# Slot tiles of a mixture-of-experts stage gathered by a list of tokens, in place of scattered and read back

## The reference

```python
def _L1_ffn_ref(x, w12, w3, router_w, expert_bias, sw1, sw2, sw3):   # E = 8, TOPK = 2
    g = x @ sw1.T                                   # shared expert, 1024 hidden
    u = x @ sw2.T
    shared_out = silu(g) * u @ sw3.T
    scores = sigmoid(x @ router_w.T)
    _, top_idx = top_k(scores + expert_bias, TOPK)
    top_scores = take_along_axis(scores, top_idx, axis=-1)
    top_scores = top_scores / (top_scores.sum(-1, keepdims=True) + 1e-09)
    combine = zeros((T, E)).at[arange(T)[:, None], flat_idx].add(flat_sc)
    h12 = einsum('td,ehd->teh', flat_x, w12)        # every expert: 128 hidden
    h1, h2 = split(h12, 2, axis=-1)
    out_e = einsum('teh,edh->ted', silu(h1) * h2, w3)
    return shared_out + einsum('ted,te->td', out_e, combine)
```

## Time and profile before

| | us |
|---|---|
| median of 3 runs | 472.29 (470.79 to 473.45) |
| profiled execution, its own time | 470.29 |
| its span, first to last instruction | 468.2 |
| TensorE busy in the span | 345.0 (74%) |
| VectorE busy | 322.6 (69%) |
| ScalarE busy | 256.0 (55%) |
| GpSimd busy | 101.4 (22%) |
| mean granted clock of TensorE | 0.874 of full speed |

### The profile page before, as it was taken

How to read it: one execution, slowest core, us unless ns; L and a number is a source line. 1 busy time by engine, 2 the same in 40 slices (tenths; PEclk the granted TensorE clock), 3 DMA queues, 4 the chain that set the end, 5 groups by cost and what they waited for, 6 DMA issues and landing times. The chain is left out here.

```text
span 468.2 us, 10194 instructions
## 1 busy us (share of the span) xinstructions
PE 345.0 (74%) x4018; PEld 270.8 (58%) x4018; DVE 322.6 (69%) x730; ACT 256.0 (55%) x527; POOL 101.4 (22%) x152
## 2 busy tenths in 40 slices
PE   1999778876599958252027788975999779888971
PEld 1544467765477747231026545654888677777861
DVE  5799997797416673999994368687895445542556
ACT  2879784466446782666223357657862336553241
POOL 6394000600000012200007400030077100003730
PEclk9999989897999997755559959997899789999986
DMA  7798000000000000000000000000012440222322
GB/s 217 243 353 294 0 0 1 0 2 0 0 3 1 3 3 1 0 1 1 0 0 3 4 3 6 3 1 1 1 45 102 132 162 1 91 104 88 99 60 90
DMA packets 18954, 24.84 MB, mean 53 GB/s; under 512 B 2582, under 2 KB 17068, under 8 KB 18860
## 3 DMA queue, kind: packets, MB, share of 16 engines
q1 hardware_dynamic: 17372, 19.99, 13.2%
q0 software_dynamic: 1536, 4.20, 2.8%
HBM read 18.02 MB, written 9.18 MB: 58 GB/s over the span
## 5 line engine op out<-in xcount | busy, mean ns | idle before, releaser
L1520 PE MATMUL ps<-ident,area 128*128 128x128 f32 x32 | 8.3, 409 | 40.6 <-DVE area L1850 40.6
L2198 PE MATMUL ps<-down_r,hidden_r 128*128 128x256 f32 x192 | 30.8, 320 | 6.7 <-DVE hidden_r L2498 3.8
L2198 PEld LDWEIGHTS ps<-down_r,hidden_r 128*128 128x128 f32 x192 | 29.4, 226 | 8.8 <-DVE hidden_r L2498 4.3
L2408 POOL DMA_INDIRECT stored<-results_dram,slots x16 | 16.7, 1045 | 67.4 <-DMA results_dram<-stored 62.8
L1520 PEld LDWEIGHTS ps<-ident,area 128*128 128x128 f32 x32 | 5.3, 202 | 43.4 <-DVE area L1850 43.4
L1847 DVE TENSOR_TENSOR third<-area 128x124 f32<-128x124 f32 (+15 forms) x31 | 29.3, 944 | 1.1
L1850 DVE TENSOR_TENSOR area<-area,third 128x124 f32<-128x124 f32 (+15 forms) x31 | 27.9, 901 | 1.1
L2230 PE MATMUL ps<-routed_up,xm_r 128*128 x138 | 23.4, 307 | 5.6 <-DVE stored L2510 2.7
L2182 PE MATMUL ps<-xm_r,gate_r 128*128 128x512 f32 x96 | 26.0, 407 | 1.0 <-ACT stored L2332 0.7
L1692 ACT ACTIVATE area<-ps,own_side 128x512 f32<-128x512 f32 (+1 forms) x16 | 15.9, 1100 | 19.1 <-PE ps L1520 19.1
L1748 ACT COPY area<-third 32x128 f32<-32x128 f32 x64 | 18.9, 295 | 13.1 <-DVE third L1894 11.9
(11 more groups left out here) (386 smaller groups left out, 987.4 us busy)
## 6 DMA issues: line engine op xcount, KB each, us to landing
stored<-in_L_ffn_sw_dram SPq DMA_DIRECT2D x3, 1024.0 KB
stored<-in_L_ffn_w_dram SPq DMA_DIRECT2D x1, 2048.0 KB
results_dram<-stored SPq DMA_DIRECT2D x2, 1024.0 KB, 4.5
stored<-rows_dram SPq DMA_DIRECT2D x1, 1920.0 KB, 8.0
x<-L_attn_hidden_state_dram SPq DMA_DIRECT2D x4, 256.0 KB, 3.6
out_dram<-x SPq DMA_DIRECT2D x4, 256.0 KB, 2.2
rows_dram<-L_attn_hidden_state_dram SPq DMA_DIRECT2D x1, 896.0 KB
stored<-rows_dram SPq DMA_DIRECT2D x1, 768.0 KB, 5.0
```

The source lines that it names most:

```text
L1520: last = nc.tensor.transpose(ps[:, bank, i * P:(i + 1) * P], inv[:, r].rearrange("p q c -> p (q c)"), ident[:])
L2198: last = nc.tensor.matmul(ps[:, t // 2, t % 2 * D:(t % 2 + 1) * D], hidden_r[:, n % 2, hp, t * P:(t + 1) * P], down_r[:, wp, a, :], start= ...
L2408: nc.gpsimd.indirect_dma_start(found[:, k, t, :], None, core.results_dram, bass.IndirectOffsetOnAxis(slots[:, k, t:t + 1], 0)) \
```

## The change

The scatter, `rows_dram`, its fill and the read-back go. In their place:

- SyncE stores `xm` to `xm_dram` (1 MB) as soon as it is normalised.
- VectorE makes two sets of 0/1 masks: `map_slots` (step 2) marks for each token and choice in which slot tile it lies (`of_tile`, multiplied by the token's number), `spread_places` (step 3) marks at which row of that tile (`in_tile`, 16 x 128 wide).
- TensorE multiplies them (`list_tokens`, step 5): 16 matmuls of 23 columns give, for each row of each slot tile, the number of its token; `keep_list` copies it to `token_of`. Padding rows get token 0, a finite row.
- GpSimd issues 23 indirect DMAs, each of which gathers a slot tile straight into SBUF, the places in a ring of 16 tiles. Tiles 16 to 22 reuse the places of tiles 0 to 6, so GpSimd waits ahead of tile 16 until results 0 to 7 have been stored (`FIRST_OUT`). TensorE waits for the gathered tiles in four parts: 0 to 3, 4 to 9, 10 to 15, 16 to 22.
- EARLY becomes 8: step 8 is computed behind the slot tiles. The weight groups are spread over steps 1 to 7, weighing moves to step 6, `keep_first` to j = 4, and one more tile is combined at the last step.

```diff
-    STEPS, EARLY, LAG = B * SH, 9, 3
-    ROW_PARTS = (0, 2, NT)
-    RESULT_PARTS = ((0, 8), (8, 16), (16, 20), (20, SLOTS))
+    STEPS, EARLY, LAG = B * SH, SH, 3
+    ROW_PARTS = (0, 4, 10, 16)
+    RESULT_PARTS = ((0, NT), (NT, 2 * NT), (2 * NT, 20), (20, SLOTS))
...
+        place = spare[:, P + 4 * NT * E + SLOTS * E:][:, 0:P]
+        RING = 2 * NT
+        rows = core.stored[:, 0:RING * D].rearrange("p (i d) -> p i d", d=D)
+        in_tile = core.stored[:, 0:2 * NT * P].rearrange("p (a r) -> p a r", a=2 * NT)
+        reached, of_tile = (core.stored[:, (NT + 2 * k) * D:(NT + 2 * k) * D + 2 * NT * (SLOTS + 1 - k)]
+                            .rearrange("p (a j) -> p a j", a=2 * NT) for k in range(2))
+        routed_hidden = core.stored[:, RING * D:RING * D + 3 * P].rearrange("p (k f) -> p k f", k=3)
...
+        XM_OUT = core.f_in_total + 16
+        FIRST_OUT, ALL_OUT = XM_OUT + 16, core.w_in_total + 16 * (len(RESULT_PARTS) - 1)
...
-        AHEAD, PER_STEP = 8, (0, 2, 2, 2, 2, 2, 2, 2, 2)
+        AHEAD, PER_STEP = 8, (0, 2, 2, 2, 2, 3, 3, 2)
...
-        COUNT_STEP, PLACE_STEP, WEIGH_STEP = 1, 1, 5
+        COUNT_STEP, PLACE_STEP, MAP_STEP, SPREAD_STEP, LIST_STEP, WEIGH_STEP = 1, 1, 2, 3, 5, 6
...
+        def slot(j):
+            return (j + NT) % RING
+
+        def part_of(j):
+            return [part for part, first in enumerate(ROW_PARTS) if first <= j][-1]
...
-        COMBINED = {STEPS - 4: (0, 1), STEPS - 3: (2, 3), STEPS - 1: (4,)}
+        COMBINED = {STEPS - 4: (0, 1), STEPS - 3: (2, 3), STEPS - 1: (4, 5)}
...
-                                                flat(both), start=k == 0, stop=k == 1,
+                                                flat(both), start=k == 0, stop=False,
                                                 skip_group_check=True)
+                    nc.tensor.matmul(ps[:, 2, 2 * NT * E:2 * NT * E + 1], upto_own, core.ones[:, 0:1], start=False,
+                                     stop=True, skip_group_check=True).then_inc(scores_done, 1)
+
+                def list_tokens():
+
+                    pe.wait_ge(routed, MAPPED)
+                    for a in range(2 * NT):
+                        last = nc.tensor.matmul(ps[:, 3, 0:SLOTS], in_tile[:, a], of_tile[:, a], start=a == 0,
+                                                stop=a == 2 * NT - 1)
...
-                        pe.wait_ge(rows_in[ROW_PARTS.index(j)], 16)
+                        pe.wait_ge(rows_in[part_of(j)], 16 * (ROW_PARTS + (SLOTS,))[part_of(j) + 1] - 16 * j)
...
-                sp.wait_ge(rows_out, 16 * 2 * NT)
-                for part, start in enumerate(ROW_PARTS):
-                    stop = (ROW_PARTS + (SLOTS,))[part + 1]
-                    sp.wait_ge(*kept(quads[1][-1] if part < 2 else groups[-1]))
-                    sp.dma_start(rows[:, start:stop], tiles(core.rows_dram)[:, start:stop, :]) \
-                        .then_inc(rows_in[part], 16)
-
+                sp.wait_ge(xm_ready, NT // 2)
+                sp.wait_ge(sem("head_on_act"), NT + NT // 2)
+                sp.dma_start(tiles(core.xm_dram), xm[:]).then_inc(xm_out, 16)
                 for start, stop in RESULT_PARTS:
                     sp.wait_ge(rows_kept, stop)
-                    sp.dma_start(tiles(core.results_dram)[:, start:stop, :], rows[:, start:stop]) \
-                        .then_inc(results_out, 16)
+                    sp.dma_start(tiles(core.results_dram)[:, start:stop, :], rows[:, slot(start):slot(stop - 1) + 1]) \
+                        .then_inc(results_out if start else xm_out, 16)
...
-                pool.wait_ge(core.f_in, core.f_in_total + core.rows_filled)
-                pool.wait_ge(routed, PLACED)
-                for t in range(NT):
-                    for k in range(2):
-                        nc.gpsimd.indirect_dma_start(core.rows_dram, bass.IndirectOffsetOnAxis(slots[:, k, t:t + 1], 0),
-                                                     xm[:, t, :], None).then_inc(rows_out, 16)
-                pool.wait_ge(results_out, 16 * (1 + len(RESULT_PARTS)))
+                pool.wait_ge(xm_out, XM_OUT)
+                pool.wait_ge(routed, LISTED)
+                for j in range(SLOTS):
+                    if j == RING:
+                        pool.wait_ge(xm_out, FIRST_OUT)
+                    nc.gpsimd.indirect_dma_start(rows[:, slot(j), :], None, core.xm_dram,
+                                                 bass.IndirectOffsetOnAxis(token_of[:, j:j + 1], 0)) \
+                        .then_inc(rows_in[part_of(j)], 16)
+                pool.wait_ge(xm_out, FIRST_OUT)
+                pool.wait_ge(results_out, ALL_OUT)
...
+                def map_slots():
+
+                    starts = steps_128[:].unsqueeze(1).to_broadcast([P, 2 * NT, SLOTS + 1])
+                    slot_ = slots_f[:].rearrange("p k t -> p (k t)")
+                    link(V.tensor_scalar(token[:], steps_128[:, 0:NT], ps[:, 2, 2 * NT * E:2 * NT * E + 1], float(P),
+                                         ALU.add, ALU.add))
+                    link(V.tensor_tensor(reached, slot_.unsqueeze(2).to_broadcast([P, 2 * NT, SLOTS + 1]), starts,
+                                         ALU.is_ge))
+                    V.tensor_tensor(of_tile, reached[:, :, 0:SLOTS], reached[:, :, 1:SLOTS + 1], ALU.subtract)
+                    link(V.tensor_reduce(tile_of[:], reached, AX_X, ALU.add))
+                    link(V.scalar_tensor_tensor(tile_of[:], tile_of[:], -float(P), slot_, ALU.mult, ALU.add))
+                    by_choice = of_tile.rearrange("p (k t) j -> p k t j", k=2)
+                    link(V.tensor_tensor(by_choice, by_choice, token[:].unsqueeze(1).unsqueeze(3)
+                                         .to_broadcast([P, 2, NT, SLOTS]), ALU.mult))
+
+                def spread_places():
+                    V.tensor_tensor(in_tile, tile_of[:].unsqueeze(2).to_broadcast([P, 2 * NT, P]),
+                                    place.unsqueeze(1).to_broadcast([P, 2 * NT, P]), ALU.is_equal).then_inc(routed, 1)
+
+                def keep_list():
+                    dve.wait_ge(scores_done, 3)
+                    V.tensor_copy(token_of[:], ps[:, 3, 0:SLOTS]).then_inc(routed, 1)
...
-                    if j == 1:
+                    if j == 4:
...
```

More of the change, by code:

```diff
@@ L108, in late_weights @@
         self.f_in = self.sem("f_in")
-        self.rows_dram, self.results_dram = (self.nc.dram_tensor(name, ((2 * NT + E - 1) * P, D), F32, kind="Internal").ap()
-                                              for name in ("rows_dram", "results_dram"))
+        self.xm_dram, self.results_dram = (self.nc.dram_tensor(name, (rows, D), F32, kind="Internal").ap()
+                                           for name, rows in (("xm_dram", N), ("results_dram", (2 * NT + E - 1) * P)))
         self.ffn_loads = [
@@ L143, in prefetch_late @@
             sp.dma_start(place, source).then_inc(self.f_in, 16)
-    def fill_rows(self, sp, rows):
-        sp.wait_ge(self.f_in, self.f_in_total)
-        for start in range(0, self.rows_dram.shape[0], N):
-            some = min(N, self.rows_dram.shape[0] - start)
-            sp.dma_start(self.rows_dram[start:start + some, :], rows[0:some, :]).then_inc(self.f_in, 16)
-            self.rows_filled += 16
     def up_tiles(self, k):
@@ L399, in _ @@
                 core.prefetch_late(sp)
-                core.fill_rows(sp, hidden)
             @block.gpsimd
@@ L2023, in expert_mixture @@
         slots = sb("slots", [P, 2, NT], U32)
+        token_of = sb("token_of_slot", [P, SLOTS], U32)
+        token = sb("token", [P, NT])
+        tile_of = sb("tile_of_slot", [P, 2 * NT])
         owner_f = sb("owner_f", [1, SLOTS])
@@ L2038, in expert_mixture @@
         compared = spare[0:1, P + 4 * NT * E:P + 4 * NT * E + SLOTS * E].rearrange("p (i e) -> p i e", e=E)
-        rows = core.stored[:, 0:SLOTS * D].rearrange("p (i d) -> p i d", d=D)
-        routed_hidden = core.stored[:, SLOTS * D:SLOTS * D + 3 * P].rearrange("p (k f) -> p k f", k=3)
+        place = spare[:, P + 4 * NT * E + SLOTS * E:][:, 0:P]
[5 more added lines that the diff above has]
+        routed_hidden = core.stored[:, RING * D:RING * D + 3 * P].rearrange("p (k f) -> p k f", k=3)
         found = core.stored[:, 8192:8192 + 2 * NT * D].rearrange("p (k t d) -> p k t d", k=2, t=NT)
@@ L2058, in expert_mixture @@
         rows_kept = sem("routed_rows_kept")
-        rows_out, rows_in = sem("rows_out"), [sem(f"rows_in_{part}") for part in range(3)]
-        results_out, results_in = rows_in[2], [sem(f"results_in_{part}") for part in range(4)]
+        rows_in, results_in = ([sem(f"{name}_in_{part}") for part in range(4)] for name in ("rows", "results"))
+        xm_out, results_out = core.f_in, core.w_in
+        XM_OUT = core.f_in_total + 16
+        FIRST_OUT, ALL_OUT = XM_OUT + 16, core.w_in_total + 16 * (len(RESULT_PARTS) - 1)
         down_done, x_ready, stored = sem("down_done"), sem("x_ready"), sem("x_stored")
@@ L2219, in turn_rows @@
```

(17 more changed lines are left out.)

11 lines of the change are left out of this document (5 added, 6 removed).

## The result

The changed kernel takes 496.35 us (median of 4 runs, 491.06 to 499.53), the kernel before 472.87 in the same job (470.79 to 474.81): ratio 1.0444, interval 1.0375 to 1.0513. Slower was forecast, but 479.5 and at most 487; the change cost 23.5 us between the medians and 21.0 by the ratio, not 7.2. The profiled execution took 491.06, the fastest of the four, with a span of 488.9, 20.7 over that of before.

The account below looks back on a forecast made before the run. TensorE was taken to set the pace, broken beside two bursts of 16 indirect DMAs. Terms -7.3 + 4.2 - 1.2 + 8.0 + 1.5 + 2.0 = +7.2 gave a median of 479.5 us, range 472 to 487.

Parts of the forecast that it names:

- Tile 0 earlier, -7.3: Start of the slot loop: tile 0 begins at 367 instead of 374.26, -7.3 us, bounds -8.0 and -4.
- The fill's removal at 0: Kernel start: the fill of `rows_dram` is waited for only by GpSimd 300 us later, so removing it changes 0.
- The clock at the loop's start, -1.2: Slot loop's start: without idle time ahead, the granted clock no longer sits at 0.78; -1.2 us (0 to -1.5).
- The ring, +8.0: Ahead of tile 16: store, seven gathers and landing take 15.2 us where 7.3 was available; +8.0, bounds 7.2 and 12.
- The step moved behind, +4.2: Behind the slot tiles: one whole shared step is added there, +4.2 us.
- the clock after the ring, +1.5: Behind the wait ahead of tile 16: slot loop work runs at a lowered clock, +1.5 us (0 to 2.8).
- The burst beside the loop, +2.0: Slot loop: row gathers issued beside it hold back ScalarE, +2.0 us, bounds 0 and 6.
- Rival C: Slot loop: the burst holds ScalarE as it did before, +6 instead of +2, 483.5 us; chance 0.20.
- Rival A: Slot loop and end: the holding back goes away and bursts cost no speed, -0.8, 471.5 us; chance 0.15.
- Rivals B and D: First: no ring wait ahead of tile 16, 468.0, chance 0.06. Second: GpSimd slow while VectorE works, +10, 489.5, chance 0.07.
- The tail at 0: From the last `down` to the kernel's end: no change forecast, 0.
- The signs of being wrong: Short gap at tile 16, tile 0 after 370, loop before tile 16 over 33 us, or last two `down` losing no 6.

Follow-up runs that it names:

- e15: e3's kernel run again: changed kernel without the ring, row and result gathers in fours, each four waited for; 473.13 us, 0.9949 of the kernel before.
- e16: e8's kernel run again beside e15: no ring, gathers in fours, the 2.9 MB of writes at the start put back; 472.13 us, ratio 0.9965.
- e5: Changed kernel with its ring kept, GpSimd waiting for every four gathers of rows and of results to land; 482.39 us, ratio 1.0164.
- e3: Changed kernel without the ring (e1), GpSimd also waiting for every four gathers of rows and of results to land; 472.68 us, ratio 0.9995.
- e10: e8 with its 23 row gathers in one unbroken run again, result gathers still in fours; 481.42 us, ratio 1.0193.
- e4: Kernel before the change, with only its 16 result gathers in fours, each four waited for; 471.61 us, ratio 0.9989.
- e1: Changed kernel without the ring: 23 places, so no gather waits for a store; gathers unbroken; 490.3 us, ratio 1.040.
- e11: e8 with its 16 result gathers in one unbroken run again, row gathers still in fours; 480.75 us, ratio 1.0172.
- e14: e10 with only 64 of each row's 256 columns gathered, a quarter of the bytes; 485.02 us, ratio 1.0274.
- e2: Changed kernel with its ring, tiles 16, 17 and 18 waited for singly and the next four in pairs; 490.64 us, ratio 1.0398.
- e13: Changed kernel with only the 2.9 MB of writes at the start put back, into a buffer nothing reads; 501.56 us, ratio 1.0603.
- e6: e3 with the 16 result gathers in two parts of eight; 473.67 us, ratio 1.0004.
- e7: e3 with the 16 result gathers in parts of twelve and four; 474.32 us, ratio 1.0001.
- e8: e3 with the 2.9 MB of writes at the start put back, into a buffer nothing reads; 470.08 us, ratio 0.9891.

## Why the prediction was wrong

The direction and the order of events were right, the size was not. By its own steps:

- **Tile 0 earlier, -7.3: measured -5.2.** The list was kept from 355.94 to 356.11 (356.05 forecast) and GpSimd started at 357.00. Tile 0 began at 369.22, not 367, inside the bound. One mis-sized part is seen: 16 float32 matmuls of 23 columns are 32 records and take 3.65 us, where I took 16 x 0.113 = 1.8. The router's row, 32 records in 3.63 us, was of 16 float32 matmuls also (8 token tiles by 2 halves of the columns); I had read each record as a matmul, and so had the list 1.8 us too short.
- **The fill's removal at 0:** not told from 0 (e15, e16).
- **The clock at the loop's start, -1.2:** not gained. From 376 to 386 the granted clock was 0.72, behind the idle stretch from 366 to 376.
- **The ring, +8.0: measured +10.1,** inside its bounds of 7.2 and 12. The store was seen after 4.66 us (398.37 to 403.03; 4.6 forecast), the seventh gather began 7.51 later (8.19), but from there to tile 16 went 5.24 us instead of 2.42. e5 against e3 prices the ring at 8.0 us by the ratios and 9.7 of the stage.
- **The step moved behind, +4.2, and the clock after the ring, +1.5:** the piece that holds both grew by 7.8, that is 2.1 over the 5.7. Most of the rest is the hold-up at the end: before, TensorE lost 6.0 us there (3.39 idle and 2.65 of clock); after, it went from 454.52 to 467.70 for a `down`, an `up` and a `down`, 13.2 us in place of 5.6, and lost 7.6. Of the clock: the first five groups from tile 16 on took 1.6 us more than at full pace (0.69, 1.65, 0.41, 0.99, 0.51 against 0.38, 0.98, 0.27, 0.60, 0.38), as forecast.
- **The burst beside the loop, +2.0 within 0 and 6; this is the step that failed,** with its twin, "the last is unchanged in length". From tile 0 to the first store 5.8 us were added where 0.8 was forecast, the largest miss of all pieces, and at the end ScalarE stood 11.51 us where before it had idled 3.85 and, three microseconds later, 2.16. With breaks after every four the changed kernel loses 9.4 us of the stage and 13.2 by the ratio (against e5), so that is what its unbroken runs cost. Rival C had the first half of it at +6 and no more than 483.5. I chose near zero because the loop issues nothing else on GpSimd or SyncE; e10 shows that the hold-up needs nothing of that kind.
- **Rival A** expected the end's hold-up to go away since it meets denser work. ScalarE's longest idle tripled instead, and TensorE's loss grew from 6.0 to 7.6 us. A's price for it stays untested: in e4 breaks took the hold-up away and delayed the results as well. A's working also has a slip, 478.7 - 7.2 for 472.3 - 0.8; both give 471.5.
- **Rivals B and D** did not come: the gap ahead of tile 16 is there, and the first 16 gathers began 1.34 us apart on average (357.00 to 377.12), not 2.55.
- **The tail at 0: +2.0.** Before, VectorE weighed results beside 24 slow `down` matmuls; after, the last `down` ends 477.35 and VectorE's own queue goes on to the end.
- **The signs of being wrong:** two of them came. From tile 0 to the gap ahead of tile 16 the loop took 36.6 us, over the 33 that were named, and the last two `down` ran at full pace, as the loss had moved ahead of them.

Terms as measured: -5.2 + 5.8 + 10.1 + 7.8 + 2.0 = 20.5, which is 13.3 over the 7.2. The profiled execution missed its forecast by 13.6 us (491.06 against 477.5) and the median by 16.9; where the other executions lost the 3.3 more, no profile shows. By the rule of the Trainium skill ("SBUF — State Buffer", section "Who interferes with whom") that only the shared port pair causes contention the burst term would be 0. The runs don't agree with the 0: 17.6 us lie between e1 and e3. They don't show what is contended for, so the rule on the ports itself is not tested.

**What the hold-up is** can be told in part. It comes with the unbroken run (e1/e3, e10, e11) and not with bytes (e14). The instruction queues' records point to where to look. In the whole profile of the changed kernel there are 33 packets on queue 8, 0.54 MB, thus 16 KB each, and 4052 + 4052 instructions of TensorE, thus 246 for each packet (register and semaphore instructions are not in that count). TensorE ran out at 454.52 + 1.34 = 455.86, and then matmuls came one by one, each behind an idle "issue". The queues' records of the changed kernel from 456.00 to 456.25 us:

```profile
q8 instruction: 1, 0.02, 24.2%
q0 software_dynamic: 1, 0.00, 0.2%
```

and from 436.0 to 455.5, with no instruction packet in it:

```profile
q0 software_dynamic: 493, 1.36, 24.1%
q1 hardware_dynamic: 400, 0.39, 5.7%
```

That looks like a TensorE that waits for its next instructions behind GpSimd's pieces. The same place of the program shows it in all five profiles of the changed kernel and its variants with 16 unbroken gathers at the end (changed kernel, e1, e2, e11, e13): TensorE stops after 10 or 11 of the 12 matmuls of the same `down`, and the packet of queue 8 is recorded 0.1 to 0.7 us later. That is 1.5 to 1.7 us after the start of that `down` in the changed kernel (456.00 to 456.25 against 454.52), but 0.2 to 0.4 us after it in e15 (444.25 to 444.50 against 444.06), where gathers go in fours and all 12 run through. The Trainium skill ("Runtime: NRT & Kernel Launch", section "Instruction fetch mechanics") has 16 KB blocks of 256 instructions, which the size of the packets agrees with. It calls the cost of crossing from one to the next "mostly hidden", which e15 agrees with and the changed kernel doesn't, if the packet is what TensorE waited for.

Three things speak against it as the whole cause. After the packet of 456.0 matmuls still come one by one for 6 us. In the kernel before, the packet at 444.75 falls into the unbroken run too, and TensorE doesn't stop there. In e14 ScalarE comes free at 388.69, and no instruction packet is recorded between 381 and 405. So a late packet is not shown as the cause, and what holds the engines stays open, as does whether number of DMAs or number of their pieces counts.

## What to carry to other kernels

Don't let GpSimd issue 16 or more indirect DMAs in one go beside a dense loop. A wait for each four to land was worth 13 us with the ring (e5) and 18 without it (e3), and in the kernel before it neither gained nor cost anything that can be told (e4). Parts of eight, or of twelve and four, did as well as fours for the results (e6, e7). When a profile shows a hold-up beside a burst that no signal explains, take the whole length of the burst as the upper bound of what a rearrangement can cost, not the idle that this arrangement happened to show. A buffer that is reused in a ring ahead of a queue of seven transfers costs store, issue and landing in a row. Look for both at once: taking the ring away alone gave 2 to 5 us (e1), breaking the runs alone 13 (e5), both together 21 to 23 (e3, e15).

## What the runs showed of the hardware

- Beside an unbroken run of 23 indirect DMAs (29 us) ScalarE stood 9.12 and 12.17 us (e14), and 19.74 in one piece in e10, and TensorE and VectorE with it. At the end, runs of 16 left it standing 11.51, 12.13 and 12.15 us, one of 12 for 6.55, and runs of four 2.23 us, the step's own pace. In the kernel before a run of 16 showed only 3.85 and 2.16; what made that one mild was not found.
- An indirect gather mostly keeps GpSimd 0.95 us, and the next starts 1.25 us after its start, with 128 KB (changed kernel) or a quarter of it (e14).
- With 16 unbroken gathers beside it TensorE stopped at the same matmul or its neighbour in five profiles of the changed kernel and its variants, just ahead of a 16 KB instruction packet. With gathers in fours it ran through (e15).
- Instructions that are the same but for 2.9 MB of writes at the start reached `owner` anywhere from 340.4 to 348.8 us. Two jobs gave ratios of 0.9995 and 0.9891 for a pair (e3, e8) that 12 executions each, side by side, put at 0.9949 and 0.9965.
